# The binary feed-forward block of a five-stage token model: the down product split in two, a maximum spread between the halves, and two clips handed to GpSimd

## The reference

```python
def _quantize_activations_groupwise(x):
    n = x.shape[0]
    gs = n // NUM_GROUPS                      # 16 images, 5 groups: 3 images each
    xq = jnp.zeros_like(x)
    for g in range(NUM_GROUPS):
        ag = x[g * gs:(g + 1) * gs]
        gamma = jnp.max(jnp.abs(ag))
        xq = xq.at[g * gs:(g + 1) * gs].set(jnp.clip(ag * QB / (gamma + EPS), -QB + EPS, QB - EPS))
    return xq

def _bitlinear(x, W, b):
    Wb = _binarize_weights_groupwise(W)
    y = jnp.einsum('btc,oc->bto', x, Wb) + b
    return _quantize_activations_groupwise(y)

h = _bitlinear(x, W1, b1)                     # 96 -> 384
h = jax.nn.gelu(h, approximate=False)
out = _bitlinear(h, W2, b2)                   # 384 -> 96
```

## Time and profile before

| | before |
|---|---|
| median of 3 runs | 1110.09 us (1109.1 to 1111.11) |
| the profiled execution's own time | 1110.88 us |
| its span | 1109.1 us |
| PE, DVE, ACT, POOL busy, share of the span | 91%, 61%, 55%, 53% |
| mean granted TensorE clock | 0.971 of full speed |

### The profile page before, as it was taken

How to read it: one execution, slowest core, us unless ns; L and a number is a source line. 1 busy time by engine, 2 the same in 40 slices (tenths; PEclk the granted TensorE clock), 3 DMA queues, 4 the chain that set the end, 5 groups by cost and what they waited for, 6 DMA issues and landing times. The chain is left out here.

```text
span 1109.1 us, 29005 instructions
## 1 busy us (share of the span) xinstructions
PE 1006.5 (91%) x11022; PEld 681.8 (61%) x11022; DVE 676.6 (61%) x1880; ACT 610.5 (55%) x1662; POOL 593.2 (53%) x788
## 2 busy tenths in 40 slices
PE   5999989799979799999999997787988988999998
PEld 2677755467745476767676765455665565566665
DVE  2899944499956355656566663576776686433332
ACT  1666633367733366666666663545665564456553
POOL 4667538477665355454545446344465545373632
PEclk9999999899989999999999998889999999999999
DMA  6500000000000000000000000000000000000000
GB/s 126 97 6 2 2 1 3 1 1 3 1 2 2 1 1 1 2 1 2 1 1 1 2 2 1 2 1 2 1 1 2 2 1 2 2 16 9 16 9 16
DMA packets 28248, 9.65 MB, mean 9 GB/s; under 512 B 26513, under 2 KB 28112, under 8 KB 28112
## 3 DMA queue, kind: packets, MB, share of 16 engines
q1 hardware_dynamic: 25088, 6.89, 3.0%
q10 hardware_dynamic: 3024, 0.92, 0.4%
HBM read 6.23 MB, written 1.57 MB: 7 GB/s over the span
## 5 line engine op out<-in xcount | busy, mean ns | idle before, releaser
L1140 POOL TENSOR_TENSOR fa_e<-fa_e,fa_rc 128x1024 f32<-128x1024 f32 x64 | 120.5, 1893 | 142.3 <-DVE fa_rc L1363 142.3
L1653 POOL TENSOR_TENSOR ca_e<-ca_e,ca_rc 128x256 f32<-128x256 f32 x96 | 76.7, 826 | 84.0 <-DVE ca_rc L1978 84.0
L1297 ACT ACTIVATE fa_e<-bank,fa_nm 128x256 f32<-128x256 f32 x256 | 118.6, 497 | 0.0
L1884 ACT ACTIVATE ca_e<-bank,ca_nm 128x128 f32<-128x128 f32 x192 | 78.0, 430 | 51.0 <-DVE ca_nm L1964 51.0
L2183 ACT ACTIVATE ex_G<-bank,e_b 128x512 f32<-128x512 f32 x96 | 64.4, 687 | 50.2 <-PE bank L137 47.5
L137 PE MATMUL bank<-hT,e_w 96*64 96x512 f32 x384 | 88.6, 596 | 0.0
L2255 DVE SCALAR_TENSOR_TENSOR X<-bank,ex_L,X 128x96 f32<-128x96 f32 x128 | 31.7, 310 | 88.9 <-PE bank L137 82.4
L1357 DVE TENSOR_REDUCE fa_nm<-bank 128x4 f32<-128x1024 f32 x64 | 75.5, 1219 | 14.6 <-PE bank L1166 14.6
L137 PEld LDWEIGHTS bank<-e_w,ex_G 128*64 128x64 f32 x1536 | 67.2, 137 | 17.2 <-issue 10.5
L167 POOL TENSOR_TENSOR ln_r<-ln_v,minus_half 128x2 f32<-128x2 f32 (+2 forms) x85 | 75.7, 890 | 0.0
L186 DVE TENSOR_TENSOR X<-X,bank 128x192 f32<-128x192 f32 (+1 forms) x72 | 30.0, 418 | 71.8 <-PE bank L137 54.2
(11 more groups left out here) (247 smaller groups left out, 2395.1 us busy)
## 6 DMA issues: line engine op xcount, KB each, us to landing
out_tokens<-X SPq DMA_DIRECT2D x8, 192.0 KB, 2.1
X<-in_x SPq DMA_DIRECT2D x14, 96.0 KB, 3.2
e_w<-in_L_ffn_w SPq DMA_DIRECT2D x2, 576.0 KB
bias0r<-in_L_conv_rpb_table ACTq DMA_DIRECT2D x16, 24.0 KB
m0w<-in_L_conv_mlp_w SPq DMA_DIRECT2D x2, 144.0 KB
m1w<-in_L_conv_w SPq DMA_DIRECT2D x2, 144.0 KB
f_w<-in_L_ffn_W SPq DMA_DIRECT2D x2, 142.5 KB
mixer<-in_mixer SPq DMA_DIRECT2D x1, 256.0 KB
```

The costliest lines, as they stand in the source:

```text
L1140: pool.tensor_tensor(e, e, r.broadcast_to([P, 4, TOK]), ALU.mult).then_inc(s["nrm"], 1)
L1297: last = act.activation(E[v % 4][:, i, c, :], bank[b + i][:, c * TOK:(c + 1) * TOK], ACT.Exp, bias=NM[v % 4][:, i, c:c + 1], accum_out=SU[ ...
L1653: last = pool.tensor_tensor(e, e, RC[u % 2][:, images, c, :].broadcast_to([P, 2, (c + 1) * P]), ALU.mult)
L1884: last = act.activation(E[u % 2][:, j, keys(c)], bank[j][:, keys(c)], ACT.Exp, bias=NM[u % 2][:, j, c:c + 1], accum_out=SU[u % 2][:, j, c: ...
```

## The change

- `down` is written as `down(g, b)`: b = 0 makes tiles 0 to 2 in bank 6, b = 1 tiles 3 to 5 in bank 7, and the spread of the inner maximum stands between them. Four of the six pieces of `up(g+1)` move into round g, ahead of the spread of the output's maximum. The warm matmuls move behind them, and write bank 0 in place of bank 2.
- `hidden_max` is three reductions, one for each block j as its two pieces arrive, and a fourth over the three results.
- On VectorE `hidden_clip(g)` moves ahead of `output(g-1)`.
- The clip of the third block of `H` goes from VectorE to GpSimd in all five groups; the output's clip goes to GpSimd in groups 0 to 3.
- GpSimd's order is now: `norm(0)`, `norm(1)`, then for each g the clip of `H`, `norm(g+2)` if there is one, and the clip of `Z` of group g-1.

```diff
@@ binary_ffn, gpsimd
+        def hidden_clip(g):
+            pool.wait_ge(s["c1"], g + 1)
+            h = H[g % 2][:, KH - 1, :]
+            pool.tensor_scalar(h, h, cc[:, 0, 1:2], cc[:, 0, 2:3], ALU.min, ALU.max).then_inc(s["clipp"], 1)
+
+        def output_clip(g):
+            pool.wait_ge(s["c2"], g + 1)
+            pool.tensor_scalar(Z[:], Z[:], cc[:, 1, 1:2], cc[:, 1, 2:3], ALU.min, ALU.max).then_inc(s["zc"], 1)
+
+        norm(0)
+        norm(1)
         for g in range(GROUPS):
-            normalise(pool, k, s, g, GT, k.Y[g % 2][:, 0:GT, :], None, g - 1)
+            hidden_clip(g)
+            if g + 2 < GROUPS:
+                norm(g + 2)
+            if g >= 1:
+                output_clip(g - 1)
         for _ in run:
             pass
@@ tensor
-            for t in range(GT):
+            for t in range(3):
                 for j in range(KH):
-                    last = halves(pe, bank[6 + t // 3][:, (t % 3) * C:(t % 3 + 1) * C], H[g % 2][:, j, t * P:(t + 1) * P], w2T[:, j, :],
+                    last = halves(pe, bank[6 + b][:, t * C:(t + 1) * C], H[g % 2][:, j, (3 * b + t) * P:(3 * b + t + 1) * P], w2T[:, j, :],
...
         run = nxt.tensor(pe)
+        up(0, 0, 4)
         for g in range(GROUPS + 1):
             if g < GROUPS:
-                up(g)
+                up(g, 4, 2)
             if g + 1 < GROUPS:
                 tokens(g + 1)
             if g >= 1:
-                down(g - 1)
+                down(g - 1, 0)
             if g < GROUPS:
-                pe.wait_ge(s["h"], 6 * (g + 1))
-                keep_warm(pe, k, bank[2][:], 4)
+                if g == 0:
+                    keep_warm(pe, k, bank[6][:], 4)
                 pe.wait_ge(s["am"], g + 1)
-                after(pe, s["z"], 2 * g)
                 spread(0, 6).then_inc(s["bc1"], 1)
+            if g >= 1:
+                down(g - 1, 1)
+            if g + 1 < GROUPS:
+                up(g + 1, 0, 4)
+                keep_warm(pe, k, bank[0][:], 4)
             if g == GROUPS:
                 next(run)
@@ vector
         def hidden_max(g):
-            dve.wait_ge(s["h"], 6 * (g + 1))
+            for j in range(KH):
+                dve.wait_ge(s["h"], 6 * g + 2 * j + 2)
+                dve.tensor_reduce(parts[:, j:j + 1], H[g % 2][:, j, :], AX.X, ALU.max, apply_absolute_value=True).then_inc(s["part"], 1)
+            dve.wait_ge(s["part"], KH * (g + 1))
             after(dve, s["bc1"], g)
-            dve.tensor_reduce(am[:, 0:1], H[g % 2][:], AX.XY, ALU.max, apply_absolute_value=True).then_inc(s["am"], 1)
+            dve.tensor_reduce(am[:, 0:1], parts[:], AX.X, ALU.max).then_inc(s["am"], 1)
...
-            for j in range(KH):
+            for j in range(KH - 1):
...
+            if g == GROUPS - 1:
+                dve.wait_ge(s["c2"], g + 1)
+                dve.tensor_scalar(Z[:], Z[:], cc[:, 1, 1:2], cc[:, 1, 2:3], ALU.min, ALU.max).then_inc(s["zc"], 1)
             dve.wait_ge(s["zc"], g + 1)
...
             if g < GROUPS:
                 hidden_max(g)
+                hidden_clip(g)
             if g >= 1:
                 output(g - 1)
-            if g < GROUPS:
-                hidden_clip(g)
-            else:
+            if g == GROUPS:
                 next(run)
```

More of the change, by code:

```diff
@@ L216 @@
 LN_SEMS = "var centred rstd y xb x bn ag mv "
-BF_SEMS = LN_SEMS + "tw twe T hT up h am bc1 ar1 c1 clip gelu down z am2 bc2 ar2 c2 zc top0 inv0 top1 inv1"
+BF_SEMS = LN_SEMS + "tw twe T hT up h part am bc1 ar1 c1 clip clipp gelu down z am2 bc2 ar2 c2 zc top0 inv0 top1 inv1"
 CA_SEMS = LN_SEMS + "init T hT ab abe abd vt v sc nm exp rec nrm et ete av ote pj oc bt"
@@ L1430, in binary_ffn @@
     am, ar, cc = sb("am", [P, 2]), sb("ar", [P, 2]), sb("cc", [P, 2, 4])
+    parts = sb("parts", [P, KH])
     half = GT * P // 2
@@ L1455, in tensor, with up, down @@
     def tensor(pe):
-        def up(g):
+        def up(g, first, count):
             pe.wait_ge(s["hT"], g + 1)
-            for j in range(KH):
-                for i in range(2):
-                    u = 2 * j + i
-                    after(pe, s["h"], 6 * g + u - 3)
-                    halves(pe, bank[2 + u % 4][:, 0:half], w1T[:, j * P:(j + 1) * P], hT[:, i * half:(i + 1) * half], start=True, stop=True).then_inc(s["up"], 1)
-        def down(g):
+            for u in range(first, first + count):
+                j, i = divmod(u, 2)
+                after(pe, s["h"], 6 * g + u - 3)
+                halves(pe, bank[2 + u % 4][:, 0:half], w1T[:, j * P:(j + 1) * P], hT[:, i * half:(i + 1) * half], start=True, stop=True).then_inc(s["up"], 1)
+        def down(g, b):
             pe.wait_ge(s["gelu"], KH * (g + 1))
@@ L1527, in scalar @@
         for g in range(GROUPS):
-            after(act, s["down"], g - 1)
+            after(act, s["down"], 2 * (g - 1))
             for j in range(KH):
```

12 lines of the change are left out of this document (7 added, 5 removed).

## The result

| | before | changed |
|---|---|---|
| median | 1111.12 us (6 runs) | 1123.58 us (6 runs, 1120.96 to 1129.02) |
| ratio to before | | 1.0134, 95% interval 1.0117 to 1.0152 |
| the profiled execution's own time | 1110.88 us | 1129.02 us |
| its span | 1109.1 us | 1127.2 us |
| mean granted TensorE clock | 0.971 | 0.959 |

The change costs 1.3% by the ratio, some 15 us of 1110; the two medians lie 12.5 us apart, 1.1%. The profiled execution of the changed kernel is the longest of its six, 5.4 us over their median, so its rows show the loss somewhat larger than the medians do. The ratios leave out two executions far above the others of their kernel, one of e9's twelve (1426 us, the others 1107 to 1113) and one of the kernel before beside e9 and e10 (1127.55 us).

A forecast was written before the change was run, and what follows sets the result against it. The binary block was taken as a ring in which engines wait for each other, no engine filling a round. Terms (a) to (d) gave +2.2, within (e)'s +12.4; with (f) and (g) +14.4 on 1110.88: 1125 us, range 1115 to 1132.

The forecast's parts named there:

- (a): First maximum of H: one reduction of 2.55 us becomes a third part of 0.85 and a join of 0.28: -1.4 us.
- (b): Second clip of H: half a down product ahead, Z's work behind, less the inner spread and a 0.65 stall: -2.1 us.
- (c): Next three rounds: VectorE waits for TensorE's later spread and GpSimd's clip; 13.8 us each, plus 0.8 for clock: +3.4 us.
- (d): Fifth clip to group 3's output scales: two clips, Z's bias and maximum, spread and scales now follow: +2.3 us.
- (e): Causal block's start: normalisations behind GpSimd's last clip of Z; projections at 769.2 for 756.76, +12.4 us, 10.2 from this order.
- (f): Projections of the causal block: TensorE idles some ten us before them and starts at a low clock: +1.5 us.
- (g): End of the six causal normalisations: they run under VectorE's last output clip and scaled sum: +0.5 us.
- the first: Rival: rounds really become short, 8.8 us, so the kernel is faster than before, 1108 us; chance 0.05.
- The second: Rival: rounds are VectorE's alone, 11.6 us, TensorE's stretch hidden; -9 from the forecast, 1116.5 us; chance 0.10.
- The third: Rival: late normalisations cost little; only +2.2 stays, 1113 us, or no difference with better rounds; chance 0.07.
- The fourth: Rival: clock falls inside every stretch and projections run wholly slow; 1130 to 1133 us; chance 0.10.

The follow-up runs named there:

- e9: e4 with ten more warm matmuls in TensorE's last wait ahead of the causal block: 1110.87 us, ratio 1.0009.
- e10: e3 with the spread of Z's maximum after two of the four ups; all clips on VectorE, normalisations early: 1110.95 us, ratio 1.0012.
- e1: The changed kernel with two of the six causal normalisations ahead of GpSimd's last clips: 1118.26 us, ratio 1.0075.
- e4: e1 with TensorE's spread of Z's maximum after two of the four ups: 1111.06 us, ratio 1.0010.
- e5: e4 with VectorE's statistics of each group moved behind the next maximum of H, into the wait for the spread: 1112.26 us, ratio 1.0021.
- e7: The changed kernel with e4's move of the spread, the causal normalisations left late: 1122.53 us, ratio 1.0109.
- e6: The changed kernel with ten warm matmuls in TensorE's wait for the join of the maximum of H: 1124.52 us, ratio 1.0127.
- e2: The kernel before, with only GpSimd's causal normalisations made to wait for the fourth group's output clip: 1121.41 us, ratio 1.0100.
- e3: The changed kernel with all clips back on VectorE, so that GpSimd only normalises: 1117.71 us, ratio 1.0071.

## Why the prediction was right

The time was forecast as 1125 us, with 1115 to 1132 as its range; the median is 1123.58. As a loss, 14.9 us were forecast, and 14.9 by the ratio or 12.5 by the medians were measured. The terms can only be held against the profiled execution, which is 5.4 us over its median, so that they agree says less of the median than of that execution. Times below are the profile's less the 0.8 us by which the block began later.

- **(a), first maximum, -1.4.** The join is 0.15 us, not the 0.28 taken, the last part 0.95, not 0.85. The first clip comes at 700.4, as forecast.
- **(b), second clip, -2.1.** At 711.35, forecast 711.6, but by luck. At full clock the first round is 9.37 us against 13.28 before, -3.9; the slow clock of the profiled execution gave 1.6 of it back (window 708 to 712 us at 0.67, in e1 at 1.00). The half down product ahead of the inner spread took 2.97 us (708.00) where e1, whose order is the same up to there, took 1.71 (707.45). e4, e5 and e7 have 9.37 us too, e9 has 10.98. The round before, from which the forecast took its times, had slow matmuls as well (0.77 in 708 to 712 us). The stall that was put at 0.65 of a possible 1.3 is the difference between 1.86 us for two clips and the 1.27 that two of the three took before: 0.6. After the first round it is hidden, as said.
- **(c), three more rounds, +3.4.** They summed to 44.1 us against 40.3: +3.8. The mechanism was the one named, VectorE waiting for TensorE's second spread (1.13, 2.78 and 3.81 us). At full clock 13.8 was forecast and 13.2 came (second round here, all three in e6): TensorE's stretch is 5.1 us by its starts (711.02 to 716.15) where single durations, which overlap, had added up to 5.8. The wait for the clip of `Z` was right (1.1 forecast, 1.07 and 0.96), though the clip itself is 0.82 us for 1.0. What the forecast didn't name is GpSimd's normalisation ahead of that clip: it adds 0.1 us here and 0.7 once the spread comes sooner (e4). The clock adds 1.8 and 2.7 us to the last two rounds, nothing to the first of the three: 4.5 where 2.4 was forecast. So the term is near because the rounds were put 1.7 too long and the clock 2.1 too short.
- **(d), +2.3.** From the fifth clip to the ready scales it is 4.8 us (756.20 to 760.98), forecast 5.0; they are ready at 760.2, as forecast.
- **(e), the main term, +12.4.** The projections begin at 770.2, forecast 769.2, before 756.8. The extra microsecond is one GpSimd subtraction that ran under VectorE's scaled sum (1.42 for 0.83), +0.6, the way from the second `Y` to the projections (1.8 us for 1.2), +0.6, less the shorter clip of `Z`. That the order of GpSimd's queue makes the projections late was right: e1 and e2 show it from both sides. Its share was put too high. From the fifth clip to the projections it is 14.8 us, in e1 6.8, so the queue makes 8.0 of it (8.5 between e7 and e4), not 10.2; in e2 it is 12.4 for 1.4 before, 11.0. The other 5.4 us of e1's 6.8 are TensorE's own part: the causal transposes stand behind a spread of Z's maximum which now starts 3.5 us after the fifth clip, where before it stood 0.8 ahead of it, and they run slow (1.94 us for 1.08). By the ratios the queue costs 6.5 us in the changed kernel (3.9 to 9.2), 11 in e2 and 11 between e7 and e4 (6.6 to 15.4), and the place of the spread 2.8 with the late normalisations (e7) or 7.2 without them (e1 to e4). So what one of the two costs depends on the other, and the ratios don't say which is the larger in the changed kernel.
- **(f), cold start, +1.5.** 4.99 us for 2.80: +2.2. Its size was within the bounds; its cause was put too narrowly. It doesn't need the gap of ten microseconds: e1, e3 and e4, whose waits there are 1.5 to 4.5 us each, have it too (4.83 to 5.27), and e9 takes it away with ten matmuls whose result nobody uses.
- **(g), +0.5.** Nothing. VectorE's last output clip and scaled sum take 0.58 and 0.82 us, as always, and the first product of probabilities on GpSimd starts 5 us after the last normalisation.

The sum is right partly by luck, because errors cancel: (b) was 1.8 too dear at full clock and the clock took 1.6 of it back, (c) without the clock, the queue's share of (e) and (g) were too high, the clock in (c), TensorE's share of (e) and (f) too low, and some 2 us of the profiled span behind the block belong to none of the terms.

Of the rivals, the first (rounds of 8.8 us) is out: the shortest of the last three rounds in any kernel of that order is 12.2, and only the first round, in which VectorE has no earlier output to quantise, comes near it (9.37). The second, that the rounds are VectorE's alone at 11.6 us, needs TensorE's stretch gone; e4 takes 2.5 us of it away (two ups, the warm matmuls) and stays at 13.2, since GpSimd's queue is next (the wait of 1.65 us against 0.95 is the 0.7 between its rounds); without that, VectorE's ring is 12.5 us (e4's last) with the hand-over and 12.2 (e10) without. 11.6 was 0.9 short, of which 0.6 is the contention. The third, that late normalisations cost little, is refuted by e2, which is the kernel before with these alone late, and 11.1 us slower. The fourth is what the profiled execution partly shows, and the median doesn't.

What the change was worth otherwise can be read from e4: everything in it, with the queue put right and the spread moved, gives what the kernel before gives. The gain of the shorter first round is in the traces; it ends at the fifth group, where TensorE's next work stands behind a spread that has become later, and starts at the low clock.

## What to carry to other kernels

Before handing an instruction to an engine with time to spare, look at what stands behind it in that engine's queue, and when it used to run: here nine clips of 0.8 to 1.4 us cost little by themselves, but the work behind them, ready 13 to 17 us ahead of need before (737.96 and 741.78, taken at 754.95), became the start of the next block. The test is one added wait in the old kernel (e2). And to shorten a ring of two engines, count the chain of both: when TensorE's share fell by 2.5 us, VectorE's wait moved from TensorE to GpSimd and the round at full clock stayed as it was. What the move did gain is that slow matmuls no longer stood where another engine waits (e7).
